# Output projection of two attention layers: plain float32 in four column tiles instead of three rounded products

## The reference, cut to what matters

```
x  = L0_attn_x
xn = layernorm(x)
x  = x + attn0(xn) + ffn0(xn)      # attn0 ends with  out @ Wo.T
xn = layernorm(x)
x  = x + attn1(xn) + ffn1(xn)      # attn1 ends with  einsum('bsh,oh->bso', ctx, w_dense) + b_dense
```

## Time and profile before

| | |
|---|---|
| median of 3 runs | 634.69 us |
| profiled execution | 634.52 us, span of its instructions 632.8 us |
| PE / DVE / ACT / POOL busy | 93% / 69% / 56% / 34% of the span |
| granted TensorE clock, mean | 0.985 |
| output projection on PE | 192 matmuls, 50.8 us busy |
| HBM | 105 GB/s over the span |

### The profile page before, as it was taken

One profiled execution on the slowest core, in us unless ns is written; L12 is line 12 of the kernel. 1 busy time (PEld: TensorE's weight loads), 2 busy tenths in 40 slices (PEclk: granted clock), 3 DMA queues, 4 the chain that ended last, 5 costly groups with the idle time before them and its releaser, 6 DMA issues.

```text
span 632.8 us, 10359 instructions
## 1 busy us (share of the span) xinstructions
PE 586.8 (93%) x3360; PEld 452.0 (71%) x3360; DVE 438.4 (69%) x815; ACT 356.3 (56%) x611; POOL 213.8 (34%) x332
## 2 busy tenths in 40 slices
PE   3788899999999999999999999897999999899985
PEld 2677677787777787677877767666777877667754
DVE  6559967656566576486897685867796887487552
ACT  2337766754564683666585564655655564474440
POOL 5703423122303331111322122443643455254231
PEclk9989999999999999999999999999899999999989
DMA  5574541353233334324543323244433353344001
GB/s 187 173 207 151 134 118 67 102 150 101 69 82 103 99 101 118 84 67 134 151 134 100 85 68 117 84 105 114 127 92 102 84 142 110 85 121 116 2 17 51
DMA packets 29805, 67.30 MB, mean 106 GB/s; under 512 B 4788, under 2 KB 17588, under 8 KB 27704
## 3 DMA queue, kind: packets, MB, share of 16 engines
q1 hardware_dynamic: 21112, 38.32, 22.2%
q0 software_dynamic: 8640, 28.32, 15.2%
HBM read 51.67 MB, written 14.68 MB: 105 GB/s over the span
## 4 chain that ended last, share of the span: by engine, by line
PE 74%; ACT 6%; DVE 6%; DMA 5%; issue 5%; POOL 2%; SPq 1%; ACTq 0%; DVEq 0%; POOLq 0%
PE banks L693 48%; PE banks L748 8%; PE banks L800 7%; PE banks L778 7%; PE banks L753 2%; DMA q_sb<-q_parts 2%; DMA raw<-in_attn 1%; PE banks L781 1%; PE banks L713 1%; ACT L917 1%; ACT probs L917 1%; ACT hid_f L937 1%; ACT L936 1%; POOL probs L649 1%; DMA q_sb<-max_t 1%
## 5 line engine op out<-in xcount | busy, mean ns | idle before, releaser
L1067 DVE TENSOR_REDUCE neg_max<-banks 128x2 f32<-128x512 f32 (+1 forms) x256 | 158.1, 620 | 150.4 <-PE banks L748 93.7
L917 ACT ACTIVATE probs<-banks 128x512 f32<-128x512 f32 (+1 forms) x256 | 137.8, 545 | 193.8 <-PE banks L778 145.6
L693 PE MATMUL banks<-xnT,w_up 128*128 128x512 f32 x576 | 157.4, 407 | 5.4 <-issue 3.7
L693 PE MATMUL banks<-w_down,hid 128*128 128x512 f32 x480 | 129.4, 403 | 4.2 <-ACT hid_f L937 2.0
L693 PEld LDWEIGHTS banks<-xnT,w_up 128*128 128x128 f32 x576 | 102.9, 192 | 33.4 <-issue 13.9
L748 PEld LDWEIGHTS banks<-k_sb,q_sb 96*128 96x128 f32 x512 | 93.6, 193 | 22.7 <-issue 5.6
L693 PEld LDWEIGHTS banks<-w_down,hid 128*128 128x128 f32 x480 | 87.0, 191 | 31.8 <-DVE neg_max L1067 6.7
L748 PE MATMUL banks<-k_sb,q_sb 96*128 96x256 f32 (+1 forms) x512 | 100.3, 278 | 4.8 <-DMA q_sb<-q_parts 4.2
L649 POOL TENSOR_SCALAR_AFFINE_SELECT probs<-probs 128x256 f32<-128x256 f32 x128 | 57.6, 450 | 111.5 <-ACT probs L917 106.6
L778 PE MATMUL banks<-q_sb,k_sb 97*128 97x512 f32 x192 | 79.3, 413 | 11.7 <-ACT probs L917 11.1
L693 PE MATMUL banks<-xnT,w_qkv 128*128 128x256 f32 x576 | 83.7, 293 | 2.3 <-DVE xnT L1011 1.4
(11 more groups left out here) (78 smaller groups left out, 629.3 us busy)
## 6 DMA issues: line engine op xcount, KB each, us to landing
q_sb<-q_parts SPq DMA_DIRECT2D x64, 256.0 KB, 4.7
raw<-in_up POOLq DMA_DIRECT2D x48, 256.0 KB, 3.0
raw<-in_down POOLq DMA_DIRECT2D x40, 256.0 KB, 3.0
q_parts<-stage SPq DMA_DIRECT2D x32, 256.0 KB, 2.6
raw<-in_attn POOLq DMA_DIRECT2D x20, 256.0 KB, 3.1
k_parts<-stage SPq DMA_DIRECT2D x16, 256.0 KB, 2.5
k_sb<-k_parts SPq DMA_DIRECT2D x16, 256.0 KB, 4.2
x_res<-in_x SPq DMA_DIRECT2D x4, 512.0 KB, 4.1
```

Source lines behind the costliest of these rows:

```text
L693: mm = nc.tensor.matmul(out_ap, lhs(a), rhs(b_), start=first and j == 0, stop=stop and j == 2, **kw)
L917: nc.scalar.activation(probs[:, i, 0:w], banks[:, ST_BANKS[k % 2], 0:w], ACT.Exp, scale=SCALES[n // B]).then_inc(exp_done, 1)
L1067: nc.vector.tensor_reduce(neg_max[:, s, 2 * g:2 * g + 2, t], banks[:, bank_of[x], :].rearrange("p (r t) -> p r t", r=2)[:, :, 0:w], AX.X, ...
```

## The change

The output projection no longer rounds and splits. `w_out` is one float32 copy of the weights, loaded by one DMA of 128 x 2048 float32 for each layer, issued by SP (`load_out`, in slot 3 of units 1 and 18). DVE's last transpose writes `ctxT` directly, in two buffers by `n % 2`; the step `ctx` and the 8 `split` pieces are gone. Each part of `wo` becomes four float32 matmuls, each with 32 tokens as the stationary operand and an output in its own quarter of the partitions. All 8 parts of a sequence's `wo` now stand in slot 1, right behind `pv`, and no longer in the fill; `COST` of a part is 460 where it was 693.

```
-COST = {... "wo": 693, ...}
+COST = {... "wo": 460, ...}
...
-        slots[5].append(("ctx", u - 1))
...
     if s == 1 and n > 0:
-        fill = parts(("wo", n - 1, 0)) + parts(("wo", n - 1, 1)) + fill
+        slots[1] += parts(("wo", n - 1, 0)) + parts(("wo", n - 1, 1))
...
-    if u == 0:
-        slots[7] += split(0, "attn", 6, 7, 8, 9)
+    if u in (1, LU + 2):
+        slots[3].append(("load_out", L))
...
-    if u in (LU + 1, LU + 2):
-        k = 6 + 2 * (u - LU - 1)
-        slots[7] += split(1, "attn", k, k + 1)
...
-        w_out = sb("w_out", [P, 2, S, D], F32R)
+        w_out = sb("w_out", [P, S, D])
...
-        ctxT = sb("ctxT", [P, 2, S, T], F32R)
+        ctxT = sb("ctxT", [P, 2, S, T])
...
+                if x[0] == "load_out":
+                    L = x[1]
+                    if L:
+                        sp_.wait_ge(wk_filled, wk["wo", B - 1, 1] + 1)
+                    sp_.dma_start(w_out[:, :, :].rearrange("p s n -> p (s n)"),
+                                  attn_w[L][:, 6 * PIECE:]).then_inc(out_w_loaded, 16)
...
-                if x[0] == "ctx":
...
-                    nc.gpsimd.tensor_tensor(ctxT[:, 1, s, :], o_t[:, :], ctxT[:, 0, s, :].bitcast(F32),
-                                            ALU.subtract).then_inc(ctx_lo, 1)
...
-                    pe.wait_ge(ctx_lo, S * n + part + 1)
+                    pe.wait_ge(o_back, S * n + part + 1)
...
-                        mm = three(banks[:, k, :], lambda h: ctxT[:, h, s, t * P:t * P + P],
-                                   lambda h: w_out[:, h, s, :], s == 0, s == S - 1)
+                        for j in range(0, P, 32):
+                            mm = nc.tensor.matmul(banks[j:j + 32, k, :], ctxT[:, n % 2, s, t * P + j:t * P + j + 32], w_out[:, s, :],
+                                                  start=s == 0, stop=s == S - 1, skip_group_check=True)
...
-                    nc.scalar.copy(ctxT[:, 0, s, :], o_t[:, :]).then_inc(ctx_hi, 1)
...
-                        if u:
-                            dve.wait_ge(ctx_lo, u)
-                        nc.vector.transpose(o_t[:, :], o_div[:, :]).then_inc(o_back, 1)
+                        n, s, f = unit(u)
+                        if n > 1 and s == 0:
+                            dve.wait_ge(wk_filled, wk["wo", n - 2, 1] + 1)
+                        nc.vector.transpose(ctxT[:, n % 2, s, :], o_div[:, :]).then_inc(o_back, 1)
```

More of the change, by code:

```diff
@@ L41 @@
 HT = 4
-COST = {"up": 681, "down": 681, "wo": 693, "qkv": 363, "xn": 440, "v": 220, "st": 233, "m": 250, "mt": 110, "pv": 995}
+COST = {"up": 681, "down": 681, "wo": 460, "qkv": 363, "xn": 440, "v": 220, "st": 233, "m": 250, "mt": 110, "pv": 995}
 def halves(x):
@@ L242, in end_slots @@
     a, b = parts(("wo", n, 0)), parts(("wo", n, 1))
-    return [[("pv", u, 1), ("norm", u, 0), ("norm", u, 1), ("norm", u, 2), ("norm", u, 3), ("ctx", u)] + a[:3] + b[:3], a[3:] + b[3:]]
+    return [[("pv", u, 1), ("norm", u, 0), ("norm", u, 1), ("norm", u, 2), ("norm", u, 3)] + a[:3] + b[:3], a[3:] + b[3:]]
 def program_order():
@@ L379, in build @@
         o_div = sb("o_div", [P, T])
-        o_t = sb("o_t", [P, T])
-        ctxT = sb("ctxT", [P, 2, S, T], F32R)
+        ctxT = sb("ctxT", [P, 2, S, T])
         qkv_v = sb("qkv_v", [P, 2, T])
@@ L430, in build @@
         o_back = sem("o_back")
-        ctx_hi = sem("ctx_hi")
-        ctx_lo = sem("ctx_lo")
+        out_w_loaded = sem("out_w_loaded")
         rot_cos = sem("rot_cos")
@@ L486, in piece @@
             if what == "attn":
[L487 to L490, removed]
+                to = [w_qkv[:, h, k // 2, 2 * (k % 2):2 * (k % 2) + 2, :].rearrange("p k n -> p (k n)") for h in range(2)]
                 return attn_w[L][:, k * PIECE:(k + 1) * PIECE], to
@@ L500, in wait_weights_free @@
             if what == "attn" and L == 1:
-                x = ("qkv", B - 1, k // 2) if k < 6 else ("wo", B - 1, 1)
-                eng.wait_ge(wk_filled, wk[x] + 1)
+                eng.wait_ge(wk_filled, wk["qkv", B - 1, k // 2] + 1)
             if what == "up":
@@ L651, in _ @@
                     done[0] = (mask_done, st_index(u - LU, i) + 1)
-                if x[0] == "ctx":
[L653 to L656, removed]
-                    nc.gpsimd.tensor_tensor(ctxT[:, 1, s, :], o_t[:, :], ctxT[:, 0, s, :].bitcast(F32),
-                                            ALU.subtract).then_inc(ctx_lo, 1)
-                    done[0] = (ctx_lo, u + 1)
                 if x[0] == "drain" and x[1][0] == "qkv" and not direct(x[1]):
@@ L805, in _ @@
                     k = work(x) if opens else bank_of[x]
-                    pe.wait_ge(ctx_lo, S * n + part + 1)
+                    pe.wait_ge(o_back, S * n + part + 1)
                     if opens:
-                        wait_low_part(pe, ("split", n // B, "attn", 9))
+                        pe.wait_ge(out_w_loaded, 16 * (n // B + 1))
                     for s in mine(range(S)):
-                        mm = three(banks[:, k, :], lambda h: ctxT[:, h, s, t * P:t * P + P],
-                                   lambda h: w_out[:, h, s, :], s == 0, s == S - 1)
+                        for j in range(0, P, 32):
+                            mm = nc.tensor.matmul(banks[j:j + 32, k, :], ctxT[:, n % 2, s, t * P + j:t * P + j + 32], w_out[:, s, :],
+                                                  start=s == 0, stop=s == S - 1, skip_group_check=True)
                     if closes:
```

## The result

The changed kernel takes 637.76 us (median of 7 runs, 634.88 to 640.18), the kernel before 633.03 us beside it (7 runs, 626.76 to 635.83). The ratio is 1.0086, with a 95% interval of 1.0044 to 1.0128. In a later session it was 1.0106 (1.0062 to 1.0149). The ratios compare fast executions alone; in that later session three of the kernel before's 17, at 636 to 637 us, count as slow and are left out, and with them its two ratios (this one and that of e9_full_width_spread) would be 0.3% lower. So the change costs 0.8 to 1.1%, 5 to 7 us. The sign was forecast; the size, 648 us with a range from 638, was more than twice too large.

The account below looks back on a forecast made before the run. The prediction took PE to bound the kernel, nearly so in layer 1 with DVE next. It summed 634.5 + 13.6 - 5.0 - 1.0 + 6.4 = 648.5 and forecast 648 us, 2.1% slower, range 638 to 659 us.

Parts of the forecast that it names:

- The projection on PE: Eight projection blocks on PE: 7.25 us each against 5.55 before, at 0.906 us a part; +13.6 us (+10.8 to +19.6).
- my lower bound: In the projection blocks, a part costs its columns alone, 0.86 us; the blocks then add +10.8 us.
- Rival D: In the projection blocks, the array drains after every part: 1.00 us a part, blocks +19.6, total 654.5 us; chance 11%.
- rival A: In the projection blocks, float32 matmul halves run beside each other: 0.46 us a part, total 618 us; chance 5%.
- The bare slots: Behind each block PE waits for ACT and DVE: 1.3 us in layer 1, 0.4 in layer 0; +6.4 us (0 to +14).
- The upper bound: Behind each block of layer 1, PE waits 3 us: two table loads and an exponential, 3.8 us, beside a bare slot.
- The splits: Three PE waits, 5.6 us in all, where ACT is held by splits of the projection's weights, go: -5.0 us (-2 to -5.6).
- The relief of ACT and POOL: In layer 1, the rest of the relief from dropped copies and subtractions gives -1 us (0 to -3).
- The weight transfer: On SP's queue, two 1 MB transfers, some 8 us each, ahead of the maxima's transfer: 0 us (0 to +2).
- The tail: At the kernel's end, PE is the chain too, so the shorter way to the last projection operand is worth nothing.
- signs of being wrong: A part costing other than 0.9 us, or PE's idle time outside the start growing over 10 us or falling.
- B: Whole kernel, no loss: blocks +10.8, split waits -5.6, ACT's and POOL's relief -3, no bare-slot waits; 636.7 us; chance 10%.

Follow-up runs that it names:

- e9_full_width_spread: Changed kernel with one full-width float32 matmul a part, projection back in the fill between score tiles, planner's cost 872: 634.51 us, ratio 1.0056 to the kernel before.
- e2: Kernel before without the splits of the projection's weights; weights loaded by SP but not read, PE reads the bias tile instead: 626.04 us, ratio 0.9906.
- e8: Changed kernel with one float32 matmul of 128 x 128 for each part in place of four column tiles, same block: 636.80 us, ratio 1.0062.
- e3: Changed kernel with the planner told 872 in place of 460 for a part, block kept: 640.31 us, ratio 1.0118 to the kernel before.
- e6: Kernel before with its eight weight splits set apart and all 24 products of a sequence's projection in one block in slot 1: 630.67 us, ratio 0.9970.
- e5: Changed kernel with the old ctx step's 32 ACT copies and 32 POOL subtractions put back, writing an unread tile: 640.14 us, ratio 1.0095.
- changed_again: The changed kernel itself measured once more, beside the kernel before: 637.68 us, ratio 1.0106.

## Why the prediction was wrong

It was right in sign and in the mechanism of its largest term, and wrong in the size of three terms, all to the same side. At the full clock the terms are 621.7 + 10.5 (the blocks) - 4.4 (the splits, by e2) + 2.6 (the place, by e8 against e9) = 630.4, and 629.2 (± 0.9) was measured; the higher clock, which the prediction had no term for, then gives back some 2 us.

**The projection on PE, +13.6 forecast, +10.5 measured.** The step that failed is "a long run of parts without a break should go on at this rate, 2 x 0.453 = 0.906". The distance of the two fours of one `pv` set held some of the way in: the weights of its first four are loaded at 309.18, as these matmuls start, and in a block every four has its weights 0.43 us ahead. In a run the next four start 0.43 us on, and a part costs 0.86, my lower bound; the block adds its way out once, so a part is 0.87 with it. I also left out what I had named, that `pv`'s own way out is saved: 0.11 us a block. Rival D (a drain for every part) is refuted by the same rows, rival A (0.46 a part) by 6.98 us a block.

**The bare slots, +6.4 forecast, +2.6 (1.5 to 3.8) by e8 against e9.** The step that failed is "So PE stands some 0.5 to 2 us behind each block of layer 1; I take 1.3, four times". In the changed kernel PE stood behind one of the four, 0.46 us for `neg_max`, and the maxima's transfer came late, 1.8 us in all, which I had looked for behind the 1 MB transfer and not behind the blocks. The argument was a balance of ACT's and DVE's work against PE's remaining time. It counted right that ACT would stand for 7 us, but not how short the chain is that PE needs: two exponentials take 1.19 us together at 478.31 and keep pace with the two slots beside them. That the two score banks and the five work banks are what lets ACT and DVE lag is argued, not shown. e3 and e6 show that the wait is real where DVE is later: there PE stands 0.47 us behind each of the four. The upper bound also had a wrong sum: two table loads and an exponential are 2 x 1.28 + 0.6 = 3.2 us, not 3.8.

**The splits, -5.0 forecast, -6.0 by e2 (-3.8 to -8.2 by its interval).** Of the waits of 5.6 us 0.24 is left in e2. The forecast lacked the clock: behind the 3.6 us stall PE ran at the lower level for 3.4 us, and the mean clock rose in every kernel in which the splits don't crowd.

**The relief of ACT and POOL, -1 forecast.** e5 shows none by the ratio and 1.2 us at the full clock; it doesn't tell 0 from 1. **The weight transfer, 0 forecast:** the changed profile has no wait of PE for the maxima above 0.8 us; the 1 MB land in 8.1 us, as worked out.

**The tail.** Its block costs what the others do, and PE goes through it without a gap, as before; no run tests the shorter way to its operand alone.

Of the signs of being wrong that were named, one came: a part costs 0.87 us, near enough to 0.9, but PE's idle time in layer 1 (400 to 560 us) fell, from 10.3 to 7.4 us.

Of the rivals, B came nearest (636.7), by columns at 0.86 and splits regained whole. Its other two terms, bare slots for nothing and 3 us for ACT's relief, were wrong in opposite directions, so that its number fits is partly luck. I gave it 10% because I took a balance of busy times for a wait.

## What to carry to other kernels

A part costs 0.86 us as plain float32 and 0.69 as three rounded products, four passes of its columns against three; and quarter-width tiles at once take the same time as one matmul of full width. So where an output fills 128 partitions anyway, neither gains PE time, and what the rounding costs on other engines matters only where PE waits for it. Look at those waits first: here eight splits cost 5 to 6 us because they stood together before four buffers, and setting them apart gave nearly as much as leaving them out.

Before a stall is charged for engines that will be late, count what the bounding engine needs from them, bank by bank, and not their total work.

Where executions of one kernel scatter with the granted clock, compare spans with the clock taken out before a difference of 2 or 3 us is called nothing.

## What the runs showed of the hardware

- Four column tiles and full width are the same in column time: 16 steps of 0.43 us in both, at the granted clock of 1.00, and 8.21 us from `pv` to the first `m` behind the block. Going in and out of tiles costs about 0.3 us a time, which a run of tiled matmuls pays once.
- A float32 matmul of 128 x 32 x 512 has a distance of 0.45 us to its second half in a lone set (309.18 to 309.63 in the kernel before), 0.43 in a run.
- The clock fell behind a 3.6 us idle time of PE in the kernel before, and behind a wait for `q_sb<-q_parts` of about 2.3 us at 551 us. It also fell at 610 us, behind 1.33 us, in the kernel before, and stayed up in the changed kernel behind an idle time of the same length; so from 570 us on the mean was 0.96 before and 1.00 after. Executions of one kernel differ in this: in changed_again the clock did fall at 615 us, behind the same 1.34 us. The kernel before spreads over 9 us.
